# The last images' attention in a new order: one new event list, u kept twice, the attention result in its own memory, and wT copied by the vector engine

## The reference

```python
x = x + conv(_gn(x))           # up-sampling filter, leaky relu, down-sampling filter, per channel
t = tokens(x)                  # 16 images of 1024 tokens of 32 channels
t = t + attention(_ln(t))      # causal, one head of 32, softmax over 1024 keys
u = _ln(t)
logits = u @ gate_w.T + gate_b           # 16 experts
probs  = softmax(logits, over the 1024 tokens)
topv, topi = top_k(probs, 8 tokens for each expert)
pooled[e]  = sum over the 8 tokens of topv * u[topi]
out[e]     = gelu([pooled[e], 1] @ weight1[e]) , 1 @ weight2[e]
t = t + scatter_add(topi, out[e] * topv)
```

## Time and profile before

| | |
|---|---|
| time, median of 3 runs | 364.86 us (364.76 to 365.97) |
| time of the profiled execution | 366.71 us |
| its span, first to last instruction | 364.8 us |
| mean granted TensorE clock | 0.954 of full speed |
| busy: PE, PEld | 323.3 us (89%), 249.3 us (68%) |
| busy: DVE, ACT, POOL | 258.4 us (71%), 186.6 us (51%), 127.3 us (35%) |

### The profile page before, as it was taken

The page is one execution under the profiler, slowest core; times in us unless marked ns, Lnnn a source line. Parts: engine busy times, 40 slices in busy tenths (PEclk is TensorE's granted clock), DMA queues, the critical chain, the costliest instruction groups (busy, mean ns, idle before and its releaser), DMA issues.

```text
span 364.8 us, 8376 instructions
## 1 busy us (share of the span) xinstructions
PE 323.3 (89%) x3357; PEld 249.3 (68%) x3357; DVE 258.4 (71%) x523; ACT 186.6 (51%) x257; POOL 127.3 (35%) x94
## 2 busy tenths in 40 slices
PE   2279998799999999999898998989998686996995
PEld 1168886587778778786767786858685444754894
DVE  2679779957766877859784877566988888265622
ACT  1043355457547574747664647466755647441510
POOL 6134635232444338454311374532116400043000
PEclk9999999999999999999999999999999999896655
DMA  4920000011010010101010101010103100100123
GB/s 123 195 49 3 23 22 16 15 17 31 16 18 23 8 32 2 31 2 34 15 16 2 31 0 32 2 31 5 26 15 74 34 2 6 42 2 29 47 68 88
DMA packets 35906, 11.16 MB, mean 31 GB/s; under 512 B 24431, under 2 KB 35741, under 8 KB 35869
## 3 DMA queue, kind: packets, MB, share of 16 engines
q1 hardware_dynamic: 33152, 9.98, 11.4%
q10 hardware_dynamic: 2717, 0.66, 1.3%
HBM read 5.72 MB, written 4.21 MB: 27 GB/s over the span
## 4 chain that ended last, share of the span: by engine, by line
PE 75%; DVE 10%; DMA 6%; issue 3%; ACT 3%; POOL 1%; SPq 1%; ACTq 1%; DVEq 0%; POOLq 0%
PE psB L923 14%; PE psA L923 13%; PE psB L1056 10%; PE psB L1036 8%; PE psA L1021 7%; PE psA L1114 5%; PE psA L1092 3%; PE psB L1073 2%; DVE negmax L784 2%; PE psA L1063 2%; PE psB L1039 2%; PE psA L911 2%; PE psA L1014 2%; PE psA L1024 2%; PE psB L1001 1%
## 5 line engine op out<-in xcount | busy, mean ns | idle before, releaser
L784 DVE TENSOR_REDUCE negmax<-psA 128x1 f32<-128x512 f32 (+7 forms) x128 | 90.7, 751 | 35.7 <-PE psA L1024 34.9
L596 ACT ACTIVATE Pp<-psB 128x1024 f32<-128x1024 f32 (+1 forms) x80 | 73.6, 938 | 34.9 <-PE psB L1039 30.8
L923 PE MATMUL psB<-xin,UU 128*128 128x224 f16 (+1 forms) x480 | 56.2, 276 | 0.2 <-issue 0.2
L923 PE MATMUL psA<-y,DD 128*128 128x224 f16 (+1 forms) x480 | 55.1, 273 | 0.0
L1021 PE MATMUL psA<-zK,yQ 128*128 128x512 f16 (+1 forms) x192 | 46.9, 326 | 7.1 <-DVE negmax L784 2.2
L923 PEld LDWEIGHTS psB<-xin,UU 128*128 128x128 f16 x480 | 46.9, 99 | 7.9 <-DVE xin L725 0.5
L1036 PE MATMUL psB<-yQ,zK 128*128 128x512 f16 (+1 forms) x192 | 47.2, 330 | 5.1 <-DMA yQ<-rows 2.8
L923 PEld LDWEIGHTS psA<-y,DD 128*128 128x128 f16 x480 | 46.8, 98 | 5.5
L486 POOL TENSOR_TENSOR zrstd<-zrstd,power 128x8 f32<-128x8 f32 x16 | 27.2, 1700 | 53.8 <-DVE zrstd L762 53.8
L566 ACT ACTIVATE y<-psB 128x1024 f16<-128x1024 f32 x16 | 16.4, 1023 | 44.5 <-PE psB L923 44.5
L508 POOL TENSOR_TENSOR y<-y 128x1024 f16<-128x1024 f32 x16 | 34.1, 2132 | 9.6 <-ACT y L569 9.6
(11 more groups left out here) (162 smaller groups left out, 499.4 us busy)
## 6 DMA issues: line engine op xcount, KB each, us to landing
x_all<-in_x_dram SPq DMA_DIRECT2D x4, 512.0 KB, 4.3
normalised_tokens<-z SPq DMA_DIRECT2D x16, 128.0 KB, 1.8
zV<-normalised_tokens SPq DMA_DIRECT2D x64, 32.0 KB, 2.2
out_dram<-x_all SPq DMA_DIRECT2D x8, 256.0 KB, 2.3
yQ<-rows SPq DMA_DIRECT2D x32, 2.0 KB
Pp<-filter_tables ACTq DMA_DIRECT2D x4, 121.9 KB, 4.2
w_halves<-y SPq DMA_DIRECT2D x12, 32.0 KB, 1.8
cst<-shape_constants SPq DMA_DIRECT2D x1, 326.5 KB, 4.3
```

The lines of the kernel that those rows point to most:

```text
L596: nc.scalar.activation(Pp[:, n % 2, UOFF[e[2]]:UOFF[e[2]] + N], slot(e)[:, 0:N], ACT.Exp).then_inc(b_drained, 1)
L784: ins = nc.vector.tensor_reduce(negmax[:, n % 2, m - 1:m], s[:, at:at + P * m], X, ALU.max, negate=True)
L923: ins = nc.tensor.matmul(within(out_cols, -shift), m, within(v, shift), start=i == 0, stop=i == len(matrices) - 1)
```

## The change

Four things change.

First, the events from the values of image 11 on are written out in one list. In it the attention of images 13 to 15 stands earlier, and the gate of group 2 (`uT`, `logits`, `logit_max`, `select`, `logit_exp`, `route`, `wT`, `pool`) stands later: `uT` of group 2 moves from between the scores of image 15 to behind its `shift`. `mean` and `dev` of group 3 move ahead. `hidden` of part 0 moves behind the last `proj`. `mean` of group 2, part 1, moves from image 12's probabilities to image 13's.

Second, `u` is kept twice, so that POOL waits for `pool` of group g-2.

Third, `att` has its own memory; the wait for `logits` moves from `proj` to `uT`.

Fourth, `wT` of groups 0 to 2 uses a bank of psA and is copied by DVE; that of group 3 stays as it was. All events of psA and psB behind the first `wT` get new banks by this.

```diff
+LAST_STEP = 12
-LAST = [("prob", B - 1, 0), ("pv", B - 2), ("prob", B - 1, 1), ("wT", G - 2), ("prob", B - 1, 2), ("mean", G - 1, 0), ("pool", G - 2),
...
+LAST = [("score", 13, 2), ("z_rstd", 15), ("prob", 12, 0), ("yQ", 14), ("dev", 2, 0), ("pv", 11), ("prob", 12, 1), ("score", 13, 0), ("prob", 12, 2),
...
-ON_B = ("up", "prob", "logits", "pv", "tok", "zK", "hidden", "wT")
-A = {e: n for n, e in enumerate(e for e in EVENTS if e[0] in ON_A)}
-BU = {e: n for n, e in enumerate(e for e in EVENTS if e[0] in ON_B)}
+ON_B = ("up", "prob", "logits", "pv", "tok", "zK", "hidden")
+LAST_WT = ("wT", G - 1)
+A = {e: n for n, e in enumerate(e for e in EVENTS if e[0] in ON_A and e != LAST_WT)}
+BU = {e: n for n, e in enumerate(e for e in EVENTS if e[0] in ON_B or e == LAST_WT)}
...
-        att = uT
+        att = sb("att", [P, S])
...
-        u = sb("u", [P, KT, P])
+        u = sb("u", [P, 2, KT, P])
...
-                    if g >= 1:
-                        pool.wait_ge(a_filled, A["pool", g - 1] + 1)
+                    if g >= 2:
+                        pool.wait_ge(a_filled, A["pool", g - 2] + 1)
...
-                elif name == "wT":
-                    if n >= 1:
-                        act.wait_ge(a_filled, A["pool", n - 1] + 1)
-                    to = wT[:, :, :].rearrange("p k n -> p (k n)")
-                    if n < G - 1:
-                        nc.scalar.activation(to, slot(e)[:, 0:KT * GE], ACT.Copy).then_inc(b_drained, 1)
...
                 elif name == "proj":
-                    if n >= 1:
-                        dve.wait_ge(b_filled, BU["logits", n - 1] + 1)
...
                 elif name == "uT":
+                    if n >= 1:
+                        dve.wait_ge(b_filled, BU["logits", n - 1] + 1)
...
+                elif name == "wT" and n < G - 1:
+                    if n >= 1:
+                        dve.wait_ge(a_filled, A["pool", n - 1] + 1)
+                    nc.vector.tensor_copy(wT[:, :, :].rearrange("p k n -> p (k n)"), s[:, 0:KT * GE]).then_inc(a_drained, 1)
```

More of the change, by code:

```diff
@@ L163, in schedule @@
     events = list(FIRST)
-    for t in range(-9, B - 1):
+    for t in range(-9, LAST_STEP):
         for event in STEP:
@@ L168, in schedule @@
                 events.append(e)
-    return events + LAST
+    return [e for e in events if e not in LAST] + LAST
 EVENTS = schedule()
-ON_A = ("xT", "small", "dnT", "gn_mean", "gn_var", "proj", "score", "uT", "shift", "down", "pool", "yQ",
+ON_A = ("xT", "small", "dnT", "gn_mean", "gn_var", "proj", "score", "uT", "shift", "down", "wT", "pool", "yQ",
         "experts", "turned", "scatter")
-ON_B = ("up", "prob", "logits", "pv", "tok", "zK", "hidden", "wT")
-A = {e: n for n, e in enumerate(e for e in EVENTS if e[0] in ON_A)}
-BU = {e: n for n, e in enumerate(e for e in EVENTS if e[0] in ON_B)}
+ON_B = ("up", "prob", "logits", "pv", "tok", "zK", "hidden")
+LAST_WT = ("wT", G - 1)
+A = {e: n for n, e in enumerate(e for e in EVENTS if e[0] in ON_A and e != LAST_WT)}
+BU = {e: n for n, e in enumerate(e for e in EVENTS if e[0] in ON_B or e == LAST_WT)}
 BANKS = 4
@@ L383, in per_token, with part_of_u @@
             return v[:, 0:count * KT].rearrange("p (b k) -> p b k", b=count).unsqueeze(3).broadcast_to([P, count, KT, C])
-        def part_of_u(first, last):
-            return u[:, :, C * first:C * last].rearrange("p k (b c) -> p b k c", b=last - first)
+        def part_of_u(n, first, last):
+            return u[:, n % 2, :, C * first:C * last].rearrange("p k (b c) -> p b k c", b=last - first)
         def prob_last(n):
@@ L527, in _ @@
                         pool.wait_ge(t2_rstd, 2 * g + e[2] + 1)
-                        v = part_of_u(first, last)
+                        v = part_of_u(g, first, last)
                         nc.gpsimd.tensor_tensor(v, v, per_token(urstd[:, e[2], :], last - first), ALU.mult).then_inc(u_ready, 1)
@@ L554, in _ @@
                 name, n = e[0], e[1]
-                if e in BU and e not in (("logits", G - 1), ("wT", G - 1)):
+                if e in BU and e not in (("logits", G - 1), LAST_WT):
                     act.wait_ge(b_filled, BU[e] + 1)
@@ L609, in _ @@
                     first, last = span_of(*e[1:])
-                    nc.scalar.activation(by_image(sq_u, 0, last - first), part_of_u(first, last), ACT.Square).then_inc(t2_squared, 1)
+                    nc.scalar.activation(by_image(sq_u, 0, last - first), part_of_u(n, first, last), ACT.Square).then_inc(t2_squared, 1)
                 elif name == "logits":
@@ L816, in _ @@
                         dve.wait_ge(t2_mean, 2 * G + 1)
-                        dve.wait_ge(a_filled, A["pool", n - 1] + 1)
-                        nc.vector.tensor_tensor(part_of_u(first, last), by_image(t2_all[:, n, :], first, last), per_token(nmean[:, e[2], :], last - first),
+                        dve.wait_ge(a_filled, A["pool", n - 2] + 1)
+                        nc.vector.tensor_tensor(part_of_u(n, first, last), by_image(t2_all[:, n, :], first, last), per_token(nmean[:, e[2], :], last - first),
                                                 ALU.add).then_inc(last_centred, 1)
@@ L1088, in _ @@
                         pe.wait_ge(wT_copied, 1)
+                    else:
+                        pe.wait_ge(a_drained, A["wT", n] + 1)
                     for k in range(KT):
[L1090 to L1092 removed]
+                        if k == R and n == G - 1:
+                            pe.wait_ge(b_drained, BU[LAST_WT] + 1)
+                        ins = nc.tensor.matmul(s[:, 0:GE], u[:, n % 2, k, :], wT[:, k, :], start=k == 0, stop=k == KT - 1)
                 elif name == "hidden":
```

40 lines of the change are left out of this document (22 added, 18 removed).

## The result

| | before | changed |
|---|---|---|
| median of 4 runs each | 365.42 us (364.76 to 366.41) | 371.32 us (370.51 to 371.68) |
| profiled execution, its span | 366.71, 364.8 us | 370.98, 369.1 us |
| mean granted clock | 0.954 | 0.950 |

The ratio is 1.0152, 95% interval 1.0128 to 1.0175. The forecast, 368.0 us and slower, had the direction; the time lies above its range.

A forecast was written before the change was run, and what follows sets the result against it. The kernel was taken as bound by PE's chain, its waits and the granted clock, with little beside the chain behind image 15's values. Terms -1.7 + 2.1 + 3.3 - 0.6 = +3.1, added to 364.86, gave 368.0 us; range 362 to 370.3.

The forecast's parts named there:

- term 1: Middle of the kernel: new banks remove PE waits of 0.93 and twice 0.94 us and add smaller ones, -1.7 us.
- term 2: End of the attention and gate of group 2: image 15's values start later, +2.1 us, 1.5 either way.
- the replay: Images 12 to 15 followed marker by marker in the changed order with durations of before; image 15's values at 321.9 us.
- image 13 came 3.2 us earlier and not 5: Sign that the forecast is right: values of image 13 start some 5 us earlier than 300.6.
- the gap of over 3 us before `wT`: Sign that the forecast is right: PE idle over 3 us before wT of group 2, granted clock 0.50 in pool.
- Term 3: Clock falls after PE's idle time at 314.1 to 318.0 us, slowing pool and image 15: +3.3 us, bounds 0 and 4.9.
- the lead never comes: Rival: the 2.9 us wait for image 13's squares costs the clock, image 13 not ahead; about 370 us, chance 0.08.
- Term 4: Tail behind image 15's values: group 3's second inverse root starts 0.5 us sooner, -0.6 us, bounds 0 and -2.
- The step from the span to the median: Whole kernel: +3.1 us added to the median 364.86, giving 368.0, where the profiled execution's 366.7 would give 369.8.
- the gate was not hidden: Rival: group 2's gate fits beside images 14 and 15; 359.3 us with all the gain, 361 with half, chance 0.18.
- the clock did not hold: Rival: the gate is last but the clock holds at the end; 364.7 us, no change, chance 0.2.
- DVE is not the bound: Rival: each of three wT copies puts 0.7 us on the path; 366.1 us with a clock that holds, chance 0.04.

The follow-up runs named there:

- the old list: Changed kernel with the event list of before; u twice, att's own memory and wT on DVE stay: 364.18 us, ratio 0.9948 to the kernel before.
- the new tail: The old list with the new resources, last projection, its dev and mean ahead of hidden, group 3's second squares ahead of image 15's values: 363.64 us, ratio 0.9935.
- the 14 runs: Runs of the unchanged kernel before, made beside the experiments, with mean granted clock 0.962 or 0.963: 364.12 to 365.31 us.
- the other 43: Runs of the unchanged kernel before, made beside the experiments, with mean granted clock 0.951 to 0.958: 365.35 to 367.14 us.
- all 57: All runs of the unchanged kernel before that were made beside the experiments: median 366.1 us.
- the run with the first products: Changed kernel with nine unread products each before image 15's second score part and before wT of group 2: 368.29 us, ratio 1.0055.
- the repaired order: Changed kernel with group 2's squares behind image 13's fourth part and its gate's choice ahead: 367.36 us; with eight unread products before pool 365.39 us.
- the tail filled: Five unread products before the first way back: 361.16 us on the old list with the new tail, 363.73 us on the repaired order with products before pool.

## Why the forecast was too low

The median lies 3.4 us above the forecast (368.0, unrounded 367.96). Of this 1.85 us are the step from the profiled execution to the median, 1.2 us are the terms, and 0.3 us the changed kernel's profiled execution, which is that much below its median. First the terms against the two profiled executions, by markers of PE's timeline:

| part of the sum | forecast | measured |
|---|---|---|
| to image 12's values: term 1 and the start of term 2 | -1.7 - 1.9 = -3.6 | 285.11 - 288.51 = -3.4 |
| image 12's to image 15's values, waits | 35.3 - 31.2 = +4.1 | +4.8 |
| the same, first low stretch | 0 | +0.7 at most |
| the same, `pool` at the lower level | +1.7 | 3.65 - 1.98 = +1.7 |
| image 15's values at the lower level | +1.6 | 7.09 - 4.77 = +2.3 |
| behind them | -0.6 | 38.45 - 40.29 = -1.8 |
| sum | +3.2 (+3.1 unrounded) | +4.3 |

The second measured line is what is left of 38.45 - 31.23 = 7.22 when the next two are taken off.

*Terms 1 and 2 held.* The middle gave 1.43 us at image 11's values, and the three waits that the replay named are there: 2.90 us for image 13's third part behind the squares, the hold for the logits' copy, and `wT` behind the exp of the logits and image 15's third part. The replay was short by 0.8 us, within its 1.5 for rounded hops. Moving either cause (squares, choice of the gate) gave 2.3 to 2.8 and 1.5 us back. Of the signs, image 13 came 3.2 us earlier and not 5, and the gap of over 3 us before `wT` came as two, 1.31 us before image 15's last part and 2.08 behind it.

*Term 3 failed in its size.* It took one low stretch, "I take the same again for image 15", from a loss of 1.6 in a stretch of before that was nearly over in this window:

```profile
314.00:316.00 2.00, 1.98 (x15) 1.43 (x14) 0.00 (x0) 1.25 (x2) 0.00 (x0) 0.89 0.18 49
```

The second stretch here lasts from 318 to beyond 328 us and takes 2.3 us from image 15's values beside `pool`'s 1.7; and there is a first one behind the 2.90 us wait, 0.7 us. That makes 4.7 instead of 3.3, against a bound of 4.9. Holding the clock gave 4.3 us back. The reason given, a wait longer than both of before, is not what happened: neither of the two gaps ahead of the second stretch is as long as the 2.76 us that left the clock alone before, and with the old list that same wait cost it. The rival "the lead never comes" had this mechanism, and was wrong on its price: image 13 is still 3.2 us ahead.

*Term 4 was too small.* -0.6 was the start of the second inverse root, which does come 0.5 us sooner behind the last projection (4.85 us, before 5.38); the wait before the first way back fell by 2.10 - 1.26 = 0.84, and the new tail was worth 0.96 by the trace. The rest of the -1.8 is group 3's logits at a higher clock than before (2.76 us, before 3.16) and the like, which the bound of -2 allowed for.

*The step from the span to the median failed by the most.* The sum is one of differences from an execution of 366.71 us with a mean granted clock of 0.954. The forecast added it to 364.86, "since the terms are differences". But 364.86 is the median of three runs, two of which, 364.76 and 364.86, have times that only the 14 runs with a clock of 0.962 or 0.963 have; the profiled execution is like the other 43, at their upper end. So gains over a kernel that loses its clock were taken off the time of runs that lose less of it. Added to the profiled execution the same terms give 369.8, as the forecast itself worked out, and its range would have ended at 372.2, above the 371.32 measured. Where in the kernel those 14 runs keep the clock is not shown, because the one execution of before that was profiled is not among them. Against 366.1, the median of all 57, the changed kernel is 5.2 us slower, and what that has beyond the 4.3 us of the two traces stays open.

The other rivals fell: the gate was not hidden, the clock did not hold, and DVE is not the bound: `wT`'s copy takes 0.69 us, for 0.7 taken, and moving it to DVE with its bank was a gain.

## What to carry to other kernels

An order written out by hand is judged queue by queue: an event moved ahead on one engine takes its instructions on all others with it, and a short step that waits (here squares of 0.6 us) holds every ready step behind it. When a new order gains on one path, look at what the same queues then leave uncovered, and price the uncovered stretch with the clock that follows it, up to where the clock is back. Part of a change can be worth having without the rest: here the memory, the bank and the copy, taken together, gained, and with the new tail and five products in one wait made the fastest kernel, while the order ahead of the tail lost. And a sum of differences belongs on the execution from which its rows were read; before it is moved to a median, ask whether the runs behind the median had the same clock.

## What was not expected of the hardware

- The length of a wait does not settle whether the clock falls, nor does what PE did just before it. 2.22 us were followed by 0.50 in the profile of before, 2.21 at the same place were not with the old list; 2.76 us at an earlier place were followed by 1.00 before and by 0.52 with the old list; 2.90 us were followed by 0.63 in the changed kernel, 2.91 at the same place by 1.00 with `wT` on ACT. In the three stretches of 2 us ahead of the wait PE was busy for 2.00, 1.31 and 2.00 us in both kernels of the first pair, for 2.00, 2.00 and 1.41 (1.40) in those of the last. The Trainium skill, page "TensorE: Matmul & The Clock Gate", section "Part 1: The HAM clock gate (the "warmup" mystery)", says that the throttle goes by PE's recent activity and that the moment at which it acts is not tied to the start of the kernel, so that it differs from run to run. The pairs, alike in the activity just before the wait, do not speak against either, and agree with the second, which no run here shows by itself.
- In the run with the first products the clock fell behind `wT` and `pool`, products of 64 columns, with PE idle for 0.88 us between them only; with four products of 512 columns in that gap it stayed at 1.00. In the repaired order eight such products in the gap did not keep it: it was 0.55 while they ran.
- The way back's eight products take 2.13 us at a granted clock of 1.00 and 2.20 at 0.50, so that the expected 1.1 did not come. Loading their weights occupies PEld for most of that time (1.88 of 2 us in the window from 328 us on with the tail filled), while the turning of `u` and the logits do follow the clock.
- Clock kept in one place was partly lost in the next: with the wait before `pool` filled, image 15's values ended 2.45 us earlier and the tail was 1.35 us longer until its own wait was filled too.
